# Layer 3's Q, K and V as three fp32r products each, 64-token transposes and 1024-column reads of PSUM in a four-layer model

## The chip, the cores and the metric

The kernel runs on one core of one Trainium2 chip. The metric is the device time of one execution in microseconds. The five engines of a core run their own instruction streams and meet at semaphores: TensorE (PE, with its weight loads as PEld), VectorE (DVE), ScalarE (ACT), GpSimd (POOL) and SyncE (SP), which issues the DMAs.

## What is computed

x is (2, 1024, 256) in float32, 2048 tokens of 256 features. Four layers follow one another: L0 (cumulative attention), L1 (attention and an MLP), L2 (16 heads of 16 features) and L3 (16 heads of 64 features, then a mixture of 8 experts). The change is at the front of L3:

```python
shift = silu(t) @ W_ada.T + b_ada
h = _ln(x, ln1_g, ln1_b) + shift
qkv = (h @ Wqkv.T).reshape(b, n, 3, H, HD)          # H = 16, HD = 64: 3072 columns
q = _ln(qkv[:, :, 0].transpose(0, 2, 1, 3), qn_g, qn_b)
k = _ln(qkv[:, :, 1].transpose(0, 2, 1, 3), kn_g, kn_b)
v = qkv[:, :, 2].transpose(0, 2, 1, 3)
scores = einsum('bhnd,bhmd->bhnm', q, k) / sqrt(HD)
```

## The kernel before

The program is a row of stages with a barrier behind each. `layer3_qkv` (line 1830) is the stage that makes q, k and v of layer 3 and writes them to DRAM for the head stage that follows.

Its start norms and transposes the 2048 tokens in NC = 4 chunks of 512 with `NormTurn` (line 615): VectorE takes mean and variance (`dve_stats`, line 642) and norms (`dve_norm`, 669), TensorE transposes into two banks (`pe_turn`, 681), ScalarE applies gain and shift on the way to `out` (`act_scale`, 690). All four chunks are done before the first product.

Then it goes over T = 16 tiles of 128 tokens. Per tile TensorE makes J + 2 = 6 banks of 512 columns, each of two fp32 products (line 1897, KF = 2 halves of the features): banks 0 and 1 are q, 2 and 3 k, 4 and 5 v. ScalarE copies each q and k bank to `qk` (1924) and squares it into `sq` (1927), and copies v (1932). VectorE sums the squares per head (1964), scales (1965) and inverts (1966), ScalarE takes the root (1934), and VectorE multiplies q and k by it into `xn` (1968). The weights' columns were centred beforehand, so no mean is taken here. In the next tile TensorE transposes `xn` (`turn`, 1883; 16 transposes of 128x128, four to a bank, the two banks 0 and 1 in turn), VectorE applies the head's gain and shift (`gains`, 1958), ScalarE rounds to the fp32r high part `hi` (1917), GpSimd subtracts to get the low part `lo` (1981), and SyncE stores v, hi and lo (1856, 1863). `TURNS` puts the transposes behind banks 3, 4 and 5. `hi`, `lo` and `full` have one buffer per group j of four heads' pairs, so ScalarE waits for the group's stores of the tile before, and VectorE for its `lo`.

The order on an engine is the order in which the code issues. The centring of the weights is done by `CentredWeights` (287) inside layer 2's head stage (`NarrowPairs`, 1331), where SyncE loads `w3qkvT` (302), `w3oT` (303) and `wgateT` (305) after the first two head pairs' loads, and GpSimd centres after it has staged V of SLOTS = 4 pairs (`pool_centre`, called in `pool_program`).

Other stages already use products of parts: a value is hi + lo, both fp32r, and the product is hi x hi + hi x lo + lo x hi, by

```python
PASSES = ((0, 0), (0, 1), (1, 0))
```

for instance in the MLP of layer 1 (line 1112), and the head stage of layer 3 transposes 64 tokens at a time in two row groups (line 1247).

## Time and profile before

| | us |
|---|---|
| runs | 2328.83, 2332.14, 2342.71 |
| median | 2332.14 |
| profiled execution, its own time | 2340.13 |
| its span | 2338.4 |
| mean granted TensorE clock | 0.896 |

Busy over the span: PE 1969.7 us (84%), DVE 1423.3 (61%), ACT 1117.9 (48%), POOL 737.9 (32%). Times in a timeline are us from the span's start. A busy time counts overlapping instructions once; a mean duration holds each instruction's whole latency, so that mean times count can exceed busy. An fp32 product of 512 columns leaves two records. "[n <-X]" is n us of idleness of the engine just before, ended by X.

### The profile page before, as it was taken

To read this page: it belongs to the slowest core of one execution; us is meant where nothing else is said; L and a number is where in the kernel's file an instruction comes from. 1 tells how busy PE (TensorE), PEld (TensorE's weight loads), DVE (VectorE), ACT (ScalarE), POOL (GpSimd) and SP (SyncE) were. 2 spreads that over 40 slices of the span, in tenths; PEclk is the share of its full clock that TensorE was granted. 3 is DMA by queue.
4 is the path that set the end of the run, shared out by engine and by line. 5 is a ranking of instruction groups with operands and counts; after the bars stand their busy time and mean duration, and the time that the engine had idled before them with its cause. 6 is when DMAs were issued, how large, how long until landed. Compare 5 with 4: busy or idle time off the path is not lost. (4 is left out here: it accounts for less than half of the span.)

```text
span 2338.4 us, 34514 instructions
## 1 busy us (share of the span) xinstructions
PE 1969.7 (84%) x12926; PEld 1155.3 (49%) x12926; DVE 1423.3 (61%) x2514; ACT 1117.9 (48%) x2013; POOL 737.9 (32%) x703
## 2 busy tenths in 40 slices
PE   6988589679649999995499949999999999794776
PEld 2444367568323333331345525555555555483676
DVE  5432543453448999960756638777777777317665
ACT  1111133231214888873256538777777777303243
POOL 2221340064003000001235535444444444103476
PEclk8999799889776999995699969999999999895688
DMA  5000000100143211102036783445444444242153
GB/s 158 0 1 0 16 7 1 38 1 1 54 135 99 47 36 49 49 7 77 7 116 216 221 223 86 113 113 113 113 113 111 110 109 109 91 149 103 31 160 81
DMA packets 197254, 190.96 MB, mean 82 GB/s; under 512 B 65440, under 2 KB 155936, under 8 KB 196832
## 3 DMA queue, kind: packets, MB, share of 16 engines
q1 hardware_dynamic: 194016, 184.56, 29.4%
q0 software_dynamic: 3072, 4.20, 0.9%
q8 instruction: 103, 1.69, 0.3%
q14 instruction: 63, 0.52, 0.1%
HBM read 121.07 MB, written 67.37 MB: 81 GB/s over the span
## 5 line engine op out<-in xcount | busy, mean ns | idle before, releaser
L1293 DVE TENSOR_REDUCE l3h_nmax<-l3h_score 128x1 f32<-128x1024 f32 x256 | 313.5, 1225 | 152.7 <-PE l3h_score L1236 152.7
L1327 POOL TENSOR_SCALAR l3h_prob<-l3h_prob,l3h_inv 128x1024 f32<-128x1024 f32 x256 | 288.3, 1126 | 340.6 <-DVE l3h_inv L1299 340.6
L1516 ACT ACTIVATE l2h_pT<-l2h_score 128x512 f32<-128x512 f32 x512 | 266.3, 602 | 118.6 <-PE l2h_score L1441 116.7
L1483 DVE TENSOR_REDUCE l2h_nm<-l2h_rowb 128x1 f32<-128x1024 f32 x256 | 301.0, 1217 | 31.8 <-PE l2h_rowb L1430 31.8
L1317 ACT ACTIVATE l3h_prob<-l3h_score,l3h_nmax 128x1024 f32<-128x1024 f32 x256 | 286.1, 1117 | 48.2 <-DVE l3h_nmax L1293 13.2
L1259 PE MATMUL l3h_out<-l3h_pT,l3h_vs 128*64 128x512 f32 x1024 | 274.4, 617 | 0.0
L1236 PE MATMUL l3h_score<-l3h_K,l3h_Q 64*128 64x512 f32 x1536 | 249.1, 430 | 26.2 <-DMA l3h_K<-l_k 24.3
L1236 PEld LDWEIGHTS l3h_score<-l3h_K,l3h_Q 64*128 64x128 f32 x1536 | 125.8, 186 | 238.0 <-issue 190.1
L1430 PE MATMUL l2h_rowb<-l2h_K,l2h_Q 48*128 48x512 f32 x512 | 183.0, 470 | 40.8 <-DMA l2h_K<-l_k 29.8
L1441 PE MATMUL l2h_score<-l2h_Q,l2h_K 50*128 50x512 f32 x512 | 206.0, 491 | 3.5 <-ACT l2h_pT L1516 3.5
L1285 ACT ACTIVATE l3h_pT<-l3h_ring 128x512 f32<-128x512 f32 x256 | 152.8, 597 | 100.9 <-PE l3h_ring L1247 100.4
L1247 PEld LDWEIGHTS l3h_ring<-ident,l3h_prob 64*128 64x128 f32 x4096 | 172.1, 139 | 37.0 <-issue 8.0
L1897 PE MATMUL l3qkv_bank<-w3qkvT,l3qkv_norm_out 128*128 128x512 f32 x384 | 174.4, 598 | 0.9 <-ACT l3qkv_norm_out L690 0.9
L1430 PEld LDWEIGHTS l2h_rowb<-l2h_K,l2h_Q 48*128 48x128 f32 x512 | 81.4, 199 | 189.1 <-DVE l2h_nm L1483 140.8
L1283 DVE COPY l3h_pT<-l3h_ring 128x512 f32<-128x512 f32 x256 | 172.1, 672 | 2.0 <-PE l3h_ring L1247 2.0
L1247 PE MATMUL l3h_ring<-ident,l3h_prob 64*128 64x64 f32 x4096 | 169.3, 222 | 2.2 <-DVE l3h_pT L1283 1.8
L1453 PE MATMUL l2h_out<-l2h_pT,l2h_vs 128*32 128x512 f32 x1024 | 148.2, 654 | 0.0
L1981 POOL TENSOR_TENSOR l3qkv_lo<-l3qkv_full,l3qkv_hi 128x512 fp32r<-128x512 f32 x64 | 102.3, 1625 | 133.6 <-ACT l3qkv_hi L1917 133.6
L1441 PEld LDWEIGHTS l2h_score<-l2h_Q,l2h_K 50*128 50x128 f32 x512 | 85.8, 195 | 63.3 <-ACT l2h_pT L1516 46.5
L1897 PEld LDWEIGHTS l3qkv_bank<-w3qkvT,l3qkv_norm_out 128*128 128x128 f32 x384 | 70.2, 192 | 72.8 <-issue 71.1
L1528 POOL COPY l2h_vs<-V 128x128 f32<-128x128 f32 x32 | 8.3, 294 | 255.3 <-PE l2h_out L1453 255.3
L1958 DVE TENSOR_SCALAR l3qkv_full<-l3qkv_bank,headln 128x512 f32<-128x512 f32 x64 | 50.5, 808 | 58.6 <-PE l3qkv_bank L1883 40.1
(355 smaller groups left out, 3364.3 us busy)
## 6 DMA issues: line engine op xcount, KB each, us to landing
l3h_Q<-l_q SPq DMA_DIRECT2D x128, 256.0 KB, 4.6
l3h_K<-l_k SPq DMA_DIRECT2D x128, 128.0 KB, 4.9
l_v<-l3qkv_v SPq DMA_DIRECT2D x16, 512.0 KB, 4.1
l_q<-l3qkv_hi SPq DMA_DIRECT2D x32, 256.0 KB, 2.8
l_q<-l3qkv_lo SPq DMA_DIRECT2D x32, 256.0 KB, 2.9
l_k<-l3qkv_hi SPq DMA_DIRECT2D x32, 256.0 KB, 3.7
l_k<-l3qkv_lo SPq DMA_DIRECT2D x32, 256.0 KB, 3.7
l3h_vs<-l_v SPq DMA_DIRECT2D x32, 256.0 KB, 3.5
```

The source lines that it names most:

```text
L1236: mm = pe.matmul(self.score[t % 2][:, c * C:(c + 1) * C], self.Q[r, u, x, t * P:(t + 1) * P], self.K[r, u, y, :], start=i == 0, stop=i == 2)
L1247: mm = pe.transpose(self.ring[half][:, kk * P // 2:(kk + 1) * P // 2], self.prob[r, g % 4, kk * P:(kk + 1) * P], self.ident[r, r])
L1259: mm = pe.matmul(self.ob[n % 2][c * self.hd:(c + 1) * self.hd, :], self.vs[:, n % 2, kk, :], self.pT[:, n % 2, kk, c * C:(c + 1) * C], sta ...
L1283: eng.tensor_copy(dst, src).then_inc(self.emptied_d, 1)
L1293: dve.tensor_reduce(self.nmax[:, t % 4:t % 4 + 1], self.score[t % 2][:, :], AX.X, ALU.max, negate=True).then_inc(self.maxes, 1)
L1317: act.activation(self.prob[:, q, :], self.score[g % 2][:, :], ACT.Exp, bias=self.nmax[:, q:q + 1], accum_out=self.total[:, q:q + 1]).then_ ...
L1327: pool.tensor_scalar(self.prob[:, q, :], self.prob[:, q, :], self.inv[:, q:q + 1], self.vscale, ALU.mult, ALU.mult).then_inc(self.scaled, 1)
L1430: mm = pe.matmul(self.rowb[h][:, c * C:(c + 1) * C], self.Q[r:r + self.SPLIT, u, t * P:(t + 1) * P], self.K[r:r + self.SPLIT, u, c * C:(c ...
L1441: pe.matmul(self.score[v % 3][:, :], self.K[r:r + self.SPLIT + 2, u, k * P:(k + 1) * P], self.Q[r:r + self.SPLIT + 2, u, c * C:(c + 1) * C ...
L1483: dve.tensor_reduce(self.nm[:, mr % 2, at:at + 1], self.rowb[h][:, :], AX.X, ALU.max, negate=True).then_inc(self.maxes, 1)
L1516: act.activation(self.pT[:, g % 4, h, c * C:(c + 1) * C], self.score[v % 3][:, :], ACT.Exp).then_inc(self.exps, 1)
L1897: mm = pe.matmul(bank[2 + j][:, :], nt.out[:, c, kf, t * P:(t + 1) * P], wT[:, (kf * 6 + j) * C:(kf * 6 + j + 1) * C], start=kf == 0, stop ...
```

## The change

- The weights are split: `w3hi` and `w3lo` (fp32r) in place of `w3qkvT`. `CentredWeights` loads one half of the features at a time into `raw`, centres it, and for three pieces of 1024 columns casts to hi and subtracts to lo. The second half and the two other weights are loaded by SyncE at pair 3, and centred before pair 8's staging.
- The normed tokens are split (`NormTurnParts`): ScalarE reads each transposed bank twice (to `out` and to hi), VectorE subtracts to lo. Two chunks come before the first product, the other two in tiles 1 and 3 (`LATER`).
- Each of the 12 fp32 products of a tile becomes three of parts; q, k and v sum in two banks each, and every read of PSUM covers 1024 columns.
- The transposes of `xn` work on 64 tokens at a time in two row groups, into one two-bank tile `turns`: 16 for q, 16 for k.
- VectorE scales the k half of tile tt-1 between inverse and multiply of tile tt, and its q half after the multiply. ScalarE rounds the q half before it copies v, and the k half at the end.
- hi and lo are stored in DMAs of 8 head pairs (512 KB) rather than 4.

TensorE in the middle of a tile, before: products into the banks (`l3qkv_bank<-w3qkvT`), two records' worth at a time, and the transposes (`<-ident,l3qkv_xn`) of the tile before.

```order
L1897 MATMUL l3qkv_bank<-w3qkvT,l3qkv_norm_out 128x512 x2
L1883 MATMUL l3qkv_bank<-ident,l3qkv_xn 128x128 x4
L1897 MATMUL l3qkv_bank<-w3qkvT,l3qkv_norm_out 128x512 x2
L1883 MATMUL l3qkv_bank<-ident,l3qkv_xn 128x128 x8
L1897 MATMUL l3qkv_bank<-w3qkvT,l3qkv_norm_out 128x512 x8
```

And now, from the last k products of tile 1 to its last v products:

```order
L1939 MATMUL l3qkv_k_sum<-w3hi,l3qkv_norm_hi 128x512
L1939 MATMUL l3qkv_k_sum<-w3lo,l3qkv_norm_hi 128x512
L1939 MATMUL l3qkv_k_sum<-w3hi,l3qkv_norm_lo 128x512
L1918 MATMUL l3qkv_turns<-ident,l3qkv_xn 128x64 x16
L1939 MATMUL l3qkv_v_sum<-w3hi,l3qkv_norm_hi 128x512
L1939 MATMUL l3qkv_v_sum<-w3lo,l3qkv_norm_hi 128x512
L1939 MATMUL l3qkv_v_sum<-w3hi,l3qkv_norm_lo 128x512
L1939 MATMUL l3qkv_v_sum<-w3hi,l3qkv_norm_hi 128x512
L1939 MATMUL l3qkv_v_sum<-w3lo,l3qkv_norm_hi 128x512
L1939 MATMUL l3qkv_v_sum<-w3hi,l3qkv_norm_lo 128x512
L1918 MATMUL l3qkv_turns<-ident,l3qkv_xn 128x64 x16
L1939 MATMUL l3qkv_v_sum<-w3hi,l3qkv_norm_hi 128x512
```

The transposes came in three places and four groups; they come in two groups with six v products between them, both into `turns`.

VectorE over one tile, before (`ss` sums of squares, `full` the scaled transposes):

```order
L1964 TENSOR_REDUCE l3qkv_ss<-l3qkv_sq 128x32
L1965 TENSOR_SCALAR l3qkv_rstd<-l3qkv_ss 128x32
L1966 RECIPROCAL l3qkv_rstd<-l3qkv_rstd 128x32
L1968 TENSOR_TENSOR l3qkv_xn<-l3qkv_qk,l3qkv_rstd 128x2048
L1958 TENSOR_SCALAR l3qkv_full<-l3qkv_bank,headln 128x512 x4
```

And now (the first `full` is the k half of the tile before, the second the q half of this one):

```order
L2024 TENSOR_REDUCE l3qkv_ss<-l3qkv_sq 128x32
L2025 TENSOR_SCALAR l3qkv_rstd<-l3qkv_ss 128x32
L2026 RECIPROCAL l3qkv_rstd<-l3qkv_rstd 128x32
L2007 TENSOR_SCALAR l3qkv_full<-l3qkv_turns,headln 128x1024
L2030 TENSOR_TENSOR l3qkv_xn<-l3qkv_qk,l3qkv_rstd 128x2048
L2007 TENSOR_SCALAR l3qkv_full<-l3qkv_turns,headln 128x1024
```

One scaling has moved ahead of the multiply; it waits for TensorE's second group of transposes.

```diff
@@ -291,15 +291,19 @@
...
+        self.raw = s.sb("centre_raw", [P, self.NQ])
...
-    def sp_load(self, sp):
+        self.loaded, self.kept, self.totals, self.means, self.centred, self.rounded, self.rest = (
+            s.sem(f"centre_{n}") for n in ("loaded", "kept", "totals", "means", "centred", "rounded", "rest"))
+
+    def sp_load(self, sp, k):
+        if k >= 1:
+            sp.wait_ge(self.rest, k * 3)
+        sp.dma_start(self.raw[:, :], self.w["WqkvT"][k * P:(k + 1) * P, :]).then_inc(self.loaded, 16)
+
+    def sp_load_rest(self, sp):
         g, w = self.g, self.w
-        for k in range(KF):
-            sp.dma_start(g["w3qkvT"][:, k * self.NQ:(k + 1) * self.NQ], w["WqkvT"][k * P:(k + 1) * P, :]).then_inc(self.loaded, 16)
...
+    def pool_centre(self, pool, k):
+        pool.wait_ge(self.loaded, 16 * (k + 1))
...
+        for i in range(3):
+            at = slice(i * 2 * C, (i + 1) * 2 * C)
+            hi, lo = (self.g[n][:, k * self.NQ + i * 2 * C:k * self.NQ + (i + 1) * 2 * C] for n in ("w3hi", "w3lo"))
+            pool.tensor_copy(hi, self.raw[:, at]).then_inc(self.rounded, 1)
+            pool.wait_ge(self.rounded, 3 * k + i + 1)
+            pool.tensor_tensor(lo, self.raw[:, at], hi.bitcast(F32), ALU.subtract).then_inc(self.rest, 1)
...
-        self.side.sp_load(sp)
+        self.side.sp_load(sp, 0)
         for m in self.TURNS:
+            if m == 3:
+                self.side.sp_load(sp, 1)
+                self.side.sp_load_rest(sp)
...
-            if m == self.SLOTS:
-                self.side.pool_centre(pool)
+            if m in (self.SLOTS, 2 * self.SLOTS):
+                self.side.pool_centre(pool, m // self.SLOTS - 1)
...
+class NormTurnParts(NormTurn):
...
+        self.parts = [s.sb(f"{name}_{n}", [P, NC, KF, C], F32R) for n in ("hi", "lo")]
...
+    def act_scale(self, act, c):
+        b = c * C // S
+        if c >= self.bufs:
+            act.wait_ge(self.split, (c - self.bufs + 1) * KF)
+        for kf in range(KF):
+            act.wait_ge(self.turned, c * KF + kf + 1)
+            for to, sem in ((self.out[:, c % self.bufs, kf, :], self.written), (self.parts[0][:, c, kf, :], self.ready)):
+                act.activation(to, self.banks[kf][:, :], ACT.Identity, bias=self.shift[:, kf, b:b + 1],
+                               scale=self.gain[:, kf, b:b + 1]).then_inc(sem, 1)
+
+    def dve_split(self, dve, c):
+        for kf in range(KF):
+            dve.wait_ge(self.written, c * KF + kf + 1)
+            dve.wait_ge(self.ready, c * KF + kf + 1)
+            dve.tensor_tensor(self.parts[1][:, c, kf, :], self.out[:, c % self.bufs, kf, :],
+                              self.parts[0][:, c, kf, :].bitcast(F32), ALU.subtract).then_inc(self.split, 1)
...
-    HD, QK, J = 64, 2 * H * 64, 4
-    TURNS = {3: (0,), 4: (1,), 5: (2, 3)}
+    HD, W = 64, H * 64
+    LATER = {1: 2, 3: 3}
     with Stage(nc, sems, "l3qkv") as s:
-        X, wT, ident = g["X"], g["w3qkvT"], g["ident"]
-        bank = [s.ps(f"bank{i}") for i in range(8)]
-        nt = NormTurn(s, X, g["gain3"], g["shift3"], ident, bank[0:2], 1e-5, bufs=NC)
-        qk = s.sb("qk", [P, 2, QK])
-        sq = s.sb("sq", [P, QK])
-        xn = s.sb("xn", [P, QK])
+        X, wp, ident = g["X"], (g["w3hi"], g["w3lo"]), g["ident"]
+        tb = s.ps("turns", (P, W))
+        sumb = [s.ps(f"{n}_sum", (P, W)) for n in ("q", "k", "v")]
+        nt = NormTurnParts(s, X, g["gain3"], g["shift3"], ident, [tb[:, kf * C:(kf + 1) * C] for kf in range(KF)], 1e-5)
+        qk = s.sb("qk", [P, 2, 2 * W])
+        sq = s.sb("sq", [P, 2 * W])
+        xn = s.sb("xn", [P, 2 * W])
...
+        full = s.sb("full", [P, 2, W])
+        vsb = s.sb("v", [P, 2, W])
+        hi, lo = s.sb("hi", [P, 2, W], F32R), s.sb("lo", [P, 2, W], F32R)
...
-                        sp.wait_ge(made, n + 1)
...
-                        sp.dma_start(dst[part, n0:n0 + 8, :, at:at + P].rearrange("(j a) d s -> (a d) j s", a=2),
-                                     src[:, j, :].bitcast(F32).rearrange("p (j s) -> p j s", j=4)).then_inc(stored[j], 16)
-            for j in range(J):
-                sp.wait_ge(stored[j], T * 32)
+                        sp.wait_ge(made, 2 * tt + i + 1)
+                        sp.dma_start(g["q3k3"][i][part, b * H:(b + 1) * H, :, at:at + P].rearrange("(j a) d s -> (a d) j s", a=2),
+                                     src[:, i, :].bitcast(F32).rearrange("p (j s) -> p j s", j=8)).then_inc(stored[i], 16)
...
+            def turn(tt, i):
+                n = 2 * tt + i
+                pe.wait_ge(normed, tt + 1)
+                if n >= 1:
+                    pe.wait_ge(fulls, n)
+                for j in range(8):
+                    for h in range(2):
+                        r = slice(h * P // 2, (h + 1) * P // 2)
+                        mm = pe.transpose(tb[:, h * C + j * P // 2:h * C + (j + 1) * P // 2],
+                                          xn[r, i * W + j * P:i * W + (j + 1) * P], ident[r, r])
+                        if j == 7:
+                            mm.then_inc(turned, 1)
+
+            for c in range(2):
                 nt.pe_turn(pe, c)
-            nt.wait_ready(pe, NC - 1)
...
-                        for kf in range(KF):
-                            mm = pe.matmul(bank[2 + j][:, :], nt.out[:, c, kf, t * P:(t + 1) * P],
-                                           wT[:, (kf * 6 + j) * C:(kf * 6 + j + 1) * C], start=kf == 0, stop=kf == KF - 1)
-                        mm.then_inc(sums if j < J else vs, 1)
-                        if tt >= 1 and j in TURNS:
-                            turn(tt - 1, TURNS[j])
-                else:
-                    turn(tt - 1, range(J))
+            nt.wait_ready(pe, 1)
+            for tt in range(T):
+                c, t = divmod(tt, TC)
+                if t == 0:
+                    nt.wait_split(pe, c)
+                for j in range(6):
+                    i, half = divmod(j, 2)
+                    if tt >= 1 and half == 0:
+                        if i < 2:
+                            pe.wait_ge(squared, (tt - 1) * 2 + i + 1)
+                        else:
+                            pe.wait_ge(vc, tt)
+                    for kf in range(KF):
+                        for p_, (x, y) in enumerate(PASSES):
+                            mm = pe.matmul(sumb[i][:, half * C:(half + 1) * C], nt.parts[x][:, c, kf, t * P:(t + 1) * P],
+                                           wp[y][:, (kf * 6 + j) * C:(kf * 6 + j + 1) * C],
+                                           start=kf == 0 and p_ == 0, stop=kf == KF - 1 and p_ == 2)
+                    if half:
+                        mm.then_inc(sums if i < 2 else vs, 1)
+                    if j == 0 and tt in LATER:
+                        pe.wait_ge(fulls, 2 * (tt - 1))
+                        nt.pe_turn(pe, LATER[tt])
+                    if tt >= 1 and j == 3:
+                        if tt in LATER:
+                            nt.wait_ready(pe, LATER[tt])
+                        turn(tt - 1, 0)
+                    if tt >= 1 and j == 4:
+                        turn(tt - 1, 1)
+            for i in range(2):
+                turn(T - 1, i)
...
+            for c in range(2):
+                nt.act_root(act, c)
+                nt.act_scale(act, c)
+
+            def round_hi(tt, i):
+                act.wait_ge(fulls, 2 * tt + i + 1)
+                if tt >= 1:
+                    act.wait_ge(stored[i], tt * 32)
+                act.activation(hi[:, i, :], full[:, i, :], ACT.Copy).then_inc(his, 1)
 
             for tt in range(T):
+                if tt in LATER:
+                    nt.act_scale(act, LATER[tt])
                 if tt >= 2:
                     act.wait_ge(normed, tt - 1)
-                for j in range(J):
-                    act.wait_ge(sums, tt * J + j + 1)
-                    act.activation(qk[:, tt % 2, j * C:(j + 1) * C], bank[2 + j][:, :], ACT.Copy).then_inc(copied, 1)
-                    if tt >= 1 and j == 0:
+                for i in range(2):
+                    act.wait_ge(sums, tt * 2 + i + 1)
+                    act.activation(qk[:, tt % 2, i * W:(i + 1) * W], sumb[i][:, :], ACT.Copy).then_inc(copied, 1)
+                    if tt >= 1 and i == 0:
                         act.wait_ge(ch, 2 * tt)
-                    act.activation(sq[:, j * C:(j + 1) * C], bank[2 + j][:, :], ACT.Square).then_inc(squared, 1)
-                for i in range(2):
-                    act.wait_ge(vs, tt * 2 + i + 1)
-                    if tt >= 2 and i == 0:
-                        act.wait_ge(vstored[tt % 2], tt // 2 * 16)
-                    act.activation(vsb[:, tt % 2, i, :], bank[2 + J + i][:, :], ACT.Copy).then_inc(vc, 1)
+                    act.activation(sq[:, i * W:(i + 1) * W], sumb[i][:, :], ACT.Square).then_inc(squared, 1)
+                    if tt == 0:
+                        nt.act_root(act, 2 + i)
+                if tt >= 1:
+                    round_hi(tt - 1, 0)
+                act.wait_ge(vs, tt + 1)
+                if tt >= 2:
+                    act.wait_ge(vstored[tt % 2], tt // 2 * 16)
+                act.activation(vsb[:, tt % 2, :], sumb[2][:, :], ACT.Copy).then_inc(vc, 1)
                 act.wait_ge(inverse, tt + 1)
                 act.activation(rstd[:, tt % 2, :], rstd[:, tt % 2, :], ACT.Sqrt).then_inc(root, 1)
                 if tt >= 1:
-                    round_hi(tt - 1)
-            round_hi(T - 1)
+                    round_hi(tt - 1, 1)
+            for i in range(2):
+                round_hi(T - 1, i)
...
+            def scaled(tt, i):
+                dve.wait_ge(turned, 2 * (2 * tt + i + 1))
+                if tt >= 1:
+                    dve.wait_ge(los, 2 * (tt - 1) + i + 1)
+                dve.tensor_scalar(full[:, i, :].rearrange("p (j h q) -> p j h q", j=8, h=2),
+                                  tb[:, :].rearrange("p (h j q) -> p j h q", h=2, j=8), g["headln"][:, 2 * i:2 * i + 1],
+                                  g["headln"][:, 2 * i + 1:2 * i + 2], ALU.mult, ALU.add).then_inc(fulls, 1)
+
+            for c in range(2):
+                nt.dve_stats(dve, c)
+                nt.dve_norm(dve, c)
+            for c in range(2):
+                nt.dve_split(dve, c)
+                nt.dve_stats(dve, c + 2)
+            for c in range(2, NC):
+                nt.dve_norm(dve, c)
             for tt in range(T):
                 u = tt % 2
-                dve.wait_ge(squared, (tt + 1) * J)
+                if tt - 1 in LATER:
+                    nt.dve_split(dve, LATER[tt - 1])
+                dve.wait_ge(squared, (tt + 1) * 2)
                 step(dve.tensor_reduce(ss[:, u, :], sq[:, :].rearrange("p (n d) -> p n d", d=HD), AX.X, ALU.add))
                 step(dve.tensor_scalar(rstd[:, u, :], ss[:, u, :], 1.0 / HD, 1e-5, ALU.mult, ALU.add))
                 dve.reciprocal(rstd[:, u, :], rstd[:, u, :]).then_inc(inverse, 1)
+                if tt >= 1:
+                    scaled(tt - 1, 1)
                 dve.wait_ge(root, tt + 1)
                 dve.tensor_tensor(xn[:, :].rearrange("p (n d) -> p n d", d=HD),
                                   qk[:, u, :].rearrange("p (n d) -> p n d", d=HD),
                                   rstd[:, u, :].unsqueeze(2).broadcast_to([P, 2 * H, HD]), ALU.mult).then_inc(normed, 1)
-                gains(tt)
+                scaled(tt, 0)
+            scaled(T - 1, 1)
...
-                for j in range(J):
-                    n = tt * J + j
+                for i in range(2):
                     if tt >= 1:
-                        pool.wait_ge(stored[j], tt * 32)
-                    pool.wait_ge(his, n + 1)
-                    pool.tensor_tensor(lo[:, j, :], full[:, j, :], hi[:, j, :].bitcast(F32), ALU.subtract).then_inc(los, 1)
+                        pool.wait_ge(stored[i], tt * 32)
+                    pool.wait_ge(his, 2 * tt + i + 1)
+                    pool.tensor_tensor(lo[:, i, :], full[:, i, :], hi[:, i, :].bitcast(F32), ALU.subtract).then_inc(los, 1)
...
-                    sb(qkv3, "w3qkvT", [P, KF * 3 * H * 64])
+                    sb(qkv3, "w3hi", [P, KF * 3 * H * 64], F32R)
+                    sb(qkv3, "w3lo", [P, KF * 3 * H * 64], F32R)
```

## Rows read from the trace of the kernel before

**Rows 1.** Window: stretch, length, busy us of PE PEld DVE ACT POOL, clock, DMA share, GB/s.

```profile
1250.00:1300.00 50.00, 50.00 (x167) 25.43 (x166) 33.48 (x33) 30.40 (x63) 27.72 (x18) 1.00 0.71 220
```

**Rows 2.** Timeline of one tile: start us, us, engine, line, what; weight loads left out.

```profile
1264.53 7.03 PE L1897 MATMUL l3qkv_bank<-w3qkvT,l3qkv_norm_out 128*128 128x512 f32 x16
...
1265.75 2.28 DVE L1964 TENSOR_REDUCE l3qkv_ss<-l3qkv_sq 128x32 f32<-128x2048 f32 x1
...
1268.66 0.23 ACT L1934 ACTIVATE l3qkv_rstd<-l3qkv_rstd 128x32 f32<-128x32 f32 x1 [4.20 <-DVE l3qkv_rstd L1966]
1268.80 2.17 ACT L1917 ACTIVATE l3qkv_hi<-l3qkv_full 128x512 fp32r<-128x512 f32 x4
...
1268.92 2.29 DVE L1968 TENSOR_TENSOR l3qkv_xn<-l3qkv_qk,l3qkv_rstd 128x2048 f32<-128x2048 f32 x1 [0.30 <-ACT l3qkv_rstd L1934]
...
1269.55 6.48 POOL L1981 TENSOR_TENSOR l3qkv_lo<-l3qkv_full,l3qkv_hi 128x512 fp32r<-128x512 f32 x4 [5.57 <-ACT l3qkv_hi L1917]
...
1270.88 0.57 ACT L1924 ACTIVATE l3qkv_qk<-l3qkv_bank 128x512 f32<-128x512 f32 x1
...
1271.36 0.58 ACT L1927 ACTIVATE l3qkv_sq<-l3qkv_bank 128x512 f32<-128x512 f32 x1
...
1276.36 1.53 DVE L1958 TENSOR_SCALAR l3qkv_full<-l3qkv_bank,headln 128x512 f32<-128x512 f32 x2 [1.35 <-PE l3qkv_bank L1883]
...
1276.59 7.03 PE L1897 MATMUL l3qkv_bank<-w3qkvT,l3qkv_norm_out 128*128 128x512 f32 x16
```

**Rows 3.** Timeline, the stage's start.

```profile
1147.86 1.40 DVE L642 BATCH_NORM_STATS2 l3qkv_norm_st<-X 128x6 f32<-128x256 f32 x4 [1.15 <-PEq L51]
...
1149.87 1.37 DVE L642 BATCH_NORM_STATS2 l3qkv_norm_st<-X 128x6 f32<-128x256 f32 x4
...
1154.42 1.63 ACT L690 ACTIVATE l3qkv_norm_out<-l3qkv_bank,shift,gain 128x512 f32<-128x512 f32 x2 [2.24 <-PE l3qkv_bank L681]
...
1167.70 19.48 PE L1897 MATMUL l3qkv_bank<-w3qkvT,l3qkv_norm_out 128*128 128x512 f32 x40 [0.87 <-ACT l3qkv_norm_out L690]
...
1178.04 2.29 DVE L1964 TENSOR_REDUCE l3qkv_ss<-l3qkv_sq 128x32 f32<-128x2048 f32 x1 [13.23 <-ACT l3qkv_sq L1927]
```

**Rows 4.** Timeline: the last tile's reduction, and the next stage's first instruction.

```profile
1362.18 2.28 DVE L1964 TENSOR_REDUCE l3qkv_ss<-l3qkv_sq 128x32 f32<-128x2048 f32 x1
...
1386.49 0.49 SPq L1199 DMA_DIRECT2D l3h_Q<-l_q  x1
```

**Rows 5.** Timeline of TensorE in layer 1's MLP: products of parts, one by one.

```profile
474.62 0.63 PE L1112 MATMUL l1mlp_bank<-l1mlp_x_hi,l1mlp_w_hi 128*128 128x512 f32 x1
475.04 0.63 PE L1112 MATMUL l1mlp_bank<-l1mlp_x_lo,l1mlp_w_hi 128*128 128x512 f32 x1
...
476.20 0.39 PE L1112 MATMUL l1mlp_bank<-l1mlp_x_hi,l1mlp_w_lo 128*128 128x512 f32 x1
...
477.79 0.39 PE L1112 MATMUL l1mlp_bank<-l1mlp_x_hi,l1mlp_w_hi 128*128 128x512 f32 x1
```

**Rows 6.** Groups of instructions (busy us, mean ns); L1981: duration ns min/median/max.

```profile
L1247 PE MATMUL l3h_ring<-ident,l3h_prob 64*128 64x64 f32 x4096 | 169.3, 222 | 2.2 <-DVE l3h_pT L1283 1.8
L1317 ACT ACTIVATE l3h_prob<-l3h_score,l3h_nmax 128x1024 f32<-128x1024 f32 x256 | 286.1, 1117 | 48.2 <-DVE l3h_nmax L1293 13.2
L1293 DVE TENSOR_REDUCE l3h_nmax<-l3h_score 128x1 f32<-128x1024 f32 x256 | 313.5, 1225 | 152.7 <-PE l3h_score L1236 152.7
L318 POOL TENSOR_TENSOR l2h_centre_tree<-w3qkvT 128x1024 f32<-128x1024 f32 x2 | 4.7, 2344 | 17.6 <-DMA w3qkvT<-in_L_cond_Wqkv 17.5
L1981 POOL TENSOR_TENSOR l3qkv_lo<-l3qkv_full,l3qkv_hi x64: 1260/1267/2863, 1197.2 to 1378.0; 128x512 fp32r<-128x512 f32 x64
```

**Rows 7.** DMA issues: count, KB each, median us from issue to landing.

```profile
l_k<-l3qkv_lo SPq DMA_DIRECT2D x32, 256.0 KB, 3.7
```

**Rows 8.** Timeline of GpSimd in layer 2's head stage: staging of V for two pairs.

```profile
754.71 0.53 POOL L1528 COPY l2h_vs<-V 128x128 f32<-128x128 f32 x2 [27.69 <-PE l2h_out L1453]
775.90 0.53 POOL L1528 COPY l2h_vs<-V 128x128 f32<-128x128 f32 x2 [20.67 <-PE l2h_out L1453]
```

94 lines of the change are left out of this document (24 added, 70 removed).

## The prediction

> **What bounds the kernel now.** I read the window view first, then the timeline of one tile of the stage that the change rewrites, then the stage's start and end. The stage `layer3_qkv` stands alone between two barriers, so what it gains or loses is the kernel's. The window 1250 to 1300 us [rows 1] shows the reader one full engine, TensorE (50.00 of 50.00 us, granted clock 1.00), beside VectorE at 33.5, ScalarE at 30.4, GpSimd at 27.7 and the DMA engines at 0.71. The timeline [rows 2] shows why: a run of 16 product records starts at 1264.53, the next at 1276.59, so a tile of 128 tokens takes 12.06 us. In it lie 24 product records (two for each of the 12 fp32 products of 512 columns), of which the long run holds 16, and 16 transposes. 16 records run 7.03 us with a tail of some 0.2, so a record costs 0.43 and a product 0.86. 12 x 0.86 = 10.3 us, and the other 1.75 us are transposes, 0.11 each. The sum is the period: TensorE sets it, and nothing else does. ScalarE even waits 4.20 us a tile before its square root [rows 2].
>
> The stage lasts from 1147.86 to 1386.49, the first instruction of the next stage [rows 3, 4]. I cut it in three: 19.84 us to the first product (1167.70) and 10.34 more until VectorE has tile 0's squares (1178.04); 184.14 us for 15 tiles, from 1178.04 to 1362.18; and a tail of 24.31 us.
>
> **The products.** Each fp32 product becomes three of fp32r parts, 36 per tile. The MLP of layer 1 shows this very form (128x128 weights, 512 columns, hi and lo in turn, a new weight load each time): from 476.20 to 477.79 seven starts lie 1.59 us apart, 0.227 us each [rows 5]. So 36 x 0.227 = 8.2 us, against 10.3.
>
> **The transposes.** 16 of 128 tokens become 32 of 64. This form is in the head stage: 4096 records busy for 169.3 us, 0.041 each [rows 6], with the two row halves beside each other. 32 x 0.041 = 1.3 us. TensorE's work is 8.2 + 1.3 = 9.5 us a tile.
>
> **A new wait on TensorE.** All transposes now go through one two-bank tile, `turns`. The k half of tile tt-1 can be transposed only when VectorE has scaled the q half. Between the two stand six v products, 1.37 us. Scaling 1024 columns from PSUM takes as long: 512 columns run at 0.72 (two in 1.53, [rows 2]), and a 1024-column read of PSUM by VectorE, the head stage's maximum, lasts 1.225 [rows 6]; I take 1.25. With 0.3 us for the last transpose and the semaphores TensorE stands some 0.3 us. Behind it are queued the last v products and the next tile's q. Period by TensorE: 9.8 us.
>
> **ScalarE and VectorE.** A second loop runs through both. ScalarE copies and squares q and k (4 instructions of 1024 columns), VectorE reduces and inverts, then, new, scales the k half of the tile before, then ScalarE rounds this to its high part, and only then copies the next q. A 1024-column read of PSUM lasts 1.117 [rows 6]. Back to back they overlap: 1270.88 and 1271.36 start 0.48 apart at 512 columns [rows 2], so I take 1.0. Loop: 4 x 1.0 + 0.1, reduce to root 2.91 (1265.75 to 1268.66), scale 1.25, round 1.05 (half of 2.17), hand-overs 0.3: 9.6 us. Without the second interleaved scaling it would be 8.4. So the new order puts this loop just under TensorE's 9.8, and either may set the tile. ScalarE's own work is 7.3 us and VectorE's 7.8, inside the period.
>
> **GpSimd and the port.** The low parts become two subtractions of 1024 columns. A 1024-column TENSOR_TENSOR takes 2.34 [rows 6]. Four of 512 took 1.27 each except the one beside VectorE's two-input multiply `xn`: 2.86 at most [rows 6], starting at 1269.55, and `xn` itself still took 2.29 [rows 2]. So 4.7 us of work, plus a wait of 1.1 us behind `xn` for the k half. The q half's subtraction now lies beside the reduction; no row here shows that pair, so its extra cost is between 0 and a full 2.28 us. I take 0, because GpSimd's median beside VectorE's other work stayed at 1.27. Even 2.28 more ends before `xn` does. The Trainium skill (SBUF — State Buffer, "Who interferes with whom") has the rule that a VectorE instruction with two SBUF inputs contends with GpSimd's reads and a tensor_reduce never does, and that whoever starts first holds the port. The first half agrees with the 2.86; by the rule my 0 stands, but the order in which `xn` and a subtraction start could turn against `xn`, which is the second rival.
>
> **The stores.** Same bytes and same 512-byte pieces, in 5 DMAs a tile instead of 9. At a share of 0.71 [rows 1] they need 12.06 x 0.71 = 8.6 us, so 88% of 9.8: not the bound. The single `hi` and `lo` buffer per half must be stored before ScalarE rounds the next tile: round 1.05, wait for `xn` 1.1, subtract 2.34, hand-overs 0.1, landing. A 256 KB k store lands in 3.7 us [rows 7]; 256 KB more at this rate are 0.9, so 4.6, together 9.2 us, under 9.8 with 0.6 to spare.
>
> **The stage's start.** The stats pass of a chunk is 2.0 us (1147.86 to 1149.87, [rows 3]). Now two chunks instead of four are normed before the first product, and each bank is read twice (out and hi), each chunk's lo made by VectorE. ScalarE gets chunk 0 at 1154.42 [rows 3], 6.6 us after the start. It comes a stats pass earlier, 4 activations at 0.82 (1.63 for two) make 3.3, then TensorE's first bank of chunk 1 1.2, 3.3 more: first product some 12.4 us after the start, 7.4 earlier. Bounds: 0.5 per activation gives 10, a wait on the split 15. The chunks left out come back inside tiles 1 and 3: TensorE waits for its transposed tile to be scaled and for four activations. Going through the waits tile by tile, tile 3 loses 3.3 us and tile 1 about 1.1 (the fulls of tile 1 exist only after tile 2's inversion, 4 us into tile 3's slot. TensorE reaches tile 3's wait 1 us into it, and the transposes, activations and hand-over behind the wait run beside the q and k products.) Cost 4.4; bounds 0 and 9.
>
> **The tail.** 24.3 us now: 16 transposes and four reads in turn, then stores one behind the other. With halves of 1024 columns the same chain is 6.8 us to `xn`, 0.8 + 1.3 + 1.1 for q, 0.8 + 1.3 + 1.1 + 2.4 for k, partly waiting on stores, and 4 for the last landing: 21. Gain 3, bounds 0 and 5.
>
> **Layer 2's head stage** gets the splitting of the weights: 6 casts and 6 subtractions on GpSimd, and half of the loads at pair 3 instead of at the start. GpSimd idles 20.67 us of every 21.19 us pair and stages a pair's V three pairs ahead [rows 8]; 15 to 30 us more each time are hidden by that. SyncE's three later loads precede the stores and shifts of pair 3, which are due 10 us on. I cost it at 0; without the cover at most 5 us.
>
> **The sum.** Start -7.4; 15 tiles 184.1 to 15 x 9.8 + 4.4 = 151.4, so -32.7; tail -3. Total -43 us. The profiled execution took 2340.13, so it would take 2297. It lies 8 us above the median of the runs, 2332.14, from which the same sum gives 2289. The time asked for is that of such runs: I say 2290.
>
> **Rivals.**
> (a) The stores' loop sets the tile: landing grows to 7 us as 512 KB DMAs queue behind v. Period 1.05 + 1.1 + 2.34 + 0.1 + 7 = 11.6, +27: 2317. For it: only 0.6 us of slack and a share of 0.88. Against it: v is issued behind the k half, not ahead.
> (b) GpSimd holds the port first and `xn` waits: up to 2.4 less 0.7 of slack a tile, 11.5, +25: 2315. Against it: counted from the squares, the q half's subtraction runs from 1.1 to 3.5 us and `xn` starts at 2.91 + 1.25 = 4.2, 0.7 later.
> (c) Slower: TensorE, no longer full (it stands 0.3 to 3 us at a time), is granted 0.5, the lower of its two levels (1.2 and 2.4 GHz), through the stage. Starts at 474.62 and 475.04 are 0.42 apart [rows 5], which is 512 columns at 1.2 GHz, so 36 x 0.42 + 2.6 = 17.8 us a tile, +5.7 against before: 16 x 5.7 - 10 = +81, 2413. It decides from a mean granted clock below 9.5 / 12.7 = 0.75. Against it: now the stage shows 1.00, and waits of 0.3 us are small beside 9.5. The Trainium skill (TensorE: Matmul & The Clock Gate, "HAM oscillation — how this bites in real kernels") says that gaps in the work bring the lower level back; the longest here come at tile 3. That page and the rows differ only in how much idleness is left, so its price is (c)'s.
> (d) The change does more: both loops at TensorE's floor of 9.5, no loss in tiles 1 and 3, a start of 10 us: -4.5 -4.4 -2.4, 2279.
>
> **How the numbers follow.** Forecast 0.80, (a) 0.06, (b) 0.06, (c) 0.03, (d) 0.05. About 1% is what a measurement of this kernel can tell from no change: 2309 and 2355 here. The forecast and (d) lie below 2309, and a little of (a) and (b), less a slice of the forecast in which the period is 11: faster 0.87; same 0.10; slower 0.03. The range takes (d) with the runs' scatter of some 7 us, 2272, and on the other side (a) and (b), 2318.
>
> **What would show it.** In the changed profile: tiles 9.8 us apart with TensorE over 95% busy at clock 1.00; product starts 0.227 apart; 1024-column reads near 1.1 us on ScalarE and 1.34 on VectorE; first product 12 us into the stage; a gap of 3 us in tile 3; the stage 195 us long instead of 238.6; layer 2's head stage unchanged. I am wrong if the tile is over 11 us (look at who releases ScalarE's rounding: a DMA is (a)), if `xn` is over 2.3 us (b), or if the clock falls (c).

## The result, and the profile after

The changed kernel took 2304.4 us (median of 4 runs, 2299.20 to 2307.17), the kernel before 2331.4 beside it (median of 4). The ratio is 0.987 with a 95% interval of 0.985 to 0.989: faster by 1.3%. The forecast was 2290 with a range of 2272 to 2318. The sign and the range held. The gain is some 30 us where 43 were forecast.

The profiled execution of the changed kernel took 2303.45 us. The stage `layer3_qkv`, by the rows that answer to [rows 3, 4]:

```profile
1149.68 1.41 DVE L651 BATCH_NORM_STATS2 l3qkv_norm_st<-X 128x6 f32<-128x256 f32 x4 [1.15 <-PEq L51]
...
1157.31 0.21 ACT L668 ACTIVATE l3qkv_norm_rstd<-l3qkv_norm_rstd 128x4 f32<-128x4 f32 x1
1157.56 1.38 DVE L678 TENSOR_SCALAR l3qkv_norm_xn<-X,l3qkv_norm_mv,l3qkv_norm_rstd 128x256 f32<-128x256 f32 x4 [2.11 <-ACT l3qkv_norm_rstd L668]
...
1162.98 0.79 PE L1939 MATMUL l3qkv_q_sum<-w3hi,l3qkv_norm_hi 128*128 128x512 f32 x1 [2.02 <-ACT l3qkv_norm_hi L1857]
...
1172.92 1.38 DVE L678 TENSOR_SCALAR l3qkv_norm_xn<-X,l3qkv_norm_mv,l3qkv_norm_rstd 128x256 f32<-128x256 f32 x4 [1.40 <-ACT l3qkv_norm_rstd L668]
...
1174.22 2.28 DVE L2024 TENSOR_REDUCE l3qkv_ss<-l3qkv_sq 128x32 f32<-128x2048 f32 x1
...
1349.76 0.49 SPq L1208 DMA_DIRECT2D l3h_Q<-l_q  x1
```

The stage lasts 1349.76 - 1149.68 = 200.08 us against 238.63. The first product comes after 13.30 us (19.84 before), the first reduction 11.24 later (10.34), the last reduction stands at 1326.96, so 15 tiles take 152.74 (184.14), and the tail is 22.80 (24.31). From the next stage's first instruction to the end of the span both kernels take 951.9 us. The window that answers to [rows 1] (same columns):

```profile
1250.00:1300.00 50.00, 50.00 (x340) 38.64 (x339) 43.09 (x30) 35.06 (x40) 27.67 (x10) 1.00 0.83 260
```

TensorE is still full, at clock 1.00. One tile, in the columns of [rows 2], most product rows left out:

```profile
1253.92 0.40 PE L1939 MATMUL l3qkv_k_sum<-w3hi,l3qkv_norm_lo 128*128 128x512 f32 x1
1254.25 0.71 PE L1918 MATMUL l3qkv_turns<-ident,l3qkv_xn 64*128 64x64 f32 x16
1254.89 0.51 PE L1939 MATMUL l3qkv_v_sum<-w3hi,l3qkv_norm_hi 128*128 128x512 f32 x1
1255.23 0.39 PE L1939 MATMUL l3qkv_v_sum<-w3lo,l3qkv_norm_hi 128*128 128x512 f32 x1
...
1256.15 0.40 PE L1939 MATMUL l3qkv_v_sum<-w3hi,l3qkv_norm_lo 128*128 128x512 f32 x1
1256.33 2.29 DVE L2024 TENSOR_REDUCE l3qkv_ss<-l3qkv_sq 128x32 f32<-128x2048 f32 x1
1256.41 1.06 ACT L1966 ACTIVATE l3qkv_hi<-l3qkv_full 128x1024 fp32r<-128x1024 f32 x1
...
1256.52 0.71 PE L1918 MATMUL l3qkv_turns<-ident,l3qkv_xn 64*128 64x64 f32 x16
...
1257.50 0.39 PE L1939 MATMUL l3qkv_v_sum<-w3lo,l3qkv_norm_hi 128*128 128x512 f32 x1
...
1257.61 2.40 POOL L2043 TENSOR_TENSOR l3qkv_lo<-l3qkv_full,l3qkv_hi 128x1024 fp32r<-128x1024 f32 x1 [1.66 <-ACT l3qkv_hi L1966]
...
1258.65 1.40 DVE L2025 TENSOR_SCALAR l3qkv_rstd<-l3qkv_ss 128x32 f32<-128x32 f32 x1
...
1260.36 1.25 DVE L2007 TENSOR_SCALAR l3qkv_full<-l3qkv_turns,headln 128x1024 f32<-128x1024 f32 x1
...
1261.52 2.28 DVE L2030 TENSOR_TENSOR l3qkv_xn<-l3qkv_qk,l3qkv_rstd 128x2048 f32<-128x2048 f32 x1
1261.64 1.06 ACT L1966 ACTIVATE l3qkv_hi<-l3qkv_full 128x1024 fp32r<-128x1024 f32 x1 [0.93 <-DVE l3qkv_full L2007]
...
1266.42 2.29 DVE L2024 TENSOR_REDUCE l3qkv_ss<-l3qkv_sq 128x32 f32<-128x2048 f32 x1
```

Reductions stand 10.09 us apart, ten times in a row; 9.8 was forecast. A surprise lies in it: VectorE's `tensor_scalar` of 128x32 at 1258.65 takes 1.40 us, and ends when GpSimd's subtraction of the q half (1257.61, 2.40 us) does. In the stage's first tile, with GpSimd idle, it takes 0.18. One can walk a closed loop by these rows: reduction 2.3, the blocked instruction 1.4, reciprocal 0.3, scaling 1.3, rounding 1.0, four reads at 0.95, and the next reduction, 10.09 later. So two engines fit the period, and a busy share doesn't say which of them sets it. That was the first question for the chip.

The second was layer 2's head stage, forecast to be free. The stage before layer 3 has one long pair. Its rows, first GpSimd's and VectorE's, then the windows (the columns of [rows 1]):

```profile
829.90 3.62 POOL L327 TENSOR_TENSOR l2h_centre_raw<-l2h_centre_raw,l2h_centre_mean 128x2048 f32<-128x2048 f32 x1
...
830.32 3.23 DVE L1502 CAST l2h_nm_parts<-l2h_nm 128x16 fp32r<-128x16 f32 x1
...
834.03 5.21 SPq L1415 DMA_DIRECT2D l2h_Q<-l2h_shift  x8
...
835.16 0.49 PE L1442 MATMUL l2h_rowb<-l2h_K,l2h_Q 48*128 48x512 f32 x1 [3.52 <-DVE l2h_nm L1495]
```

```profile
827.00:831.00 4.00, 4.00 (x27) 1.24 (x27) 3.72 (x4) 3.36 (x7) 3.52 (x7) 1.00 0.00 0
831.00:835.00 4.00, 0.65 (x4) 0.21 (x4) 3.93 (x4) 1.09 (x2) 3.86 (x3) 1.00 0.00 0
835.00:839.00 4.00, 3.84 (x20) 1.85 (x20) 2.84 (x4) 1.97 (x4) 3.92 (x3) 0.66 0.02 3
839.00:843.00 4.00, 4.00 (x18) 1.57 (x17) 2.29 (x3) 2.00 (x5) 3.92 (x3) 0.50 0.01 1
843.00:847.00 4.00, 4.00 (x27) 1.21 (x26) 3.81 (x4) 3.31 (x7) 0.97 (x1) 0.98 0.24 64
```

VectorE's cast of a pair's maxima, 0.17 us in the other pairs, takes 3.23 beside GpSimd's centring of the second half of the weights. Behind it on VectorE stands the first reduction of the next maxima (`l2h_nm`), which frees the bank that TensorE fills next. So TensorE stands from 831.64 to 835.16, and then runs at a granted clock of 0.66 and 0.50 until 843. GpSimd's stagings of V are 26.63 us apart there (823.22 and 849.85) and 21.23 from one pair to the next in the steady part: 5.4 us lost, in a term that I had at 0.

### The profile page after: what moved, and what is told of

Read it like the earlier page. It is cut to its first block and busy times, and to the rows that moved or that the text cites. A ratio compares the mean times of both kernels' runs of the same rounds, so it can differ in the third digit from the quotient of the medians.

```text
span 2301.7 us, 35109 instructions
## 1 busy us (share of the span) xinstructions
PE 1931.4 (84%) x13374; PEld 1181.4 (51%) x13374; DVE 1435.9 (62%) x2490; ACT 1116.1 (48%) x1909; POOL 739.2 (32%) x683
## 5 line engine op out<-in xcount | busy, mean ns | idle before, releaser
L2043 POOL TENSOR_TENSOR l3qkv_lo<-l3qkv_full,l3qkv_hi 128x1024 fp32r<-128x1024 f32 x32 | 88.9, 2778 | 109.3 <-ACT l3qkv_hi L1966 109.3
L1705 PE MATMUL l3o_bank<-w3oT,l3o_oT 128*128 128x256 f32 x256 | 57.9, 391 | 13.0 <-DMA l3o_oT<-l_heads_out 13.0
L2419 PE MATMUL moe_up<-moe_gT_hi,moe_w1T_hi 128*128 128x256 f32 x128 | 42.9, 335 | 29.8 <-DVE moe_gT_lo L2499 24.8
L505 PE MATMUL l_bank<-l_csum,l_val 128*128 128x512 f32 x128 | 64.2, 626 | 4.0 <-DVE l_aT L590 4.0
```

## The experiments

All times of a stage are from the profile of each kernel; "tile" is the distance of two reductions in the steady part. Except for e8, each edit is made to the changed kernel alone. e1, e4 and e5 leave out terms of the products and serve for their times only.

**e1: two products of parts in place of three.** The loop over the passes in this stage:

```diff
-for p_, (x, y) in enumerate(PASSES):
+for p_, (x, y) in enumerate(((0, 0), (1, 0))):
```

> The product of the tokens' high parts with the weights' low parts is left out in layer 3's Q, K and V: 24 products a tile in place of 36. In the changed kernel the tiles stand 10.09 us apart. Theory 'port': the period is a loop of ScalarE and VectorE (reduction 2.29, tensor_scalar 1.40 behind GpSimd's subtraction, reciprocal 0.35, scaling 1.25, rounding, two copies and two squares), and TensorE has room. Then the period stays 10.1 us although 12 x 0.232 = 2.8 us of TensorE's work go. Rival 'TensorE': 8.35 of products, 1.4 of transposes and its waits set the tile, as the prediction had it; then the period falls to 8 or 9 us.

Measured: tile 9.82 us, its small `tensor_scalar` 1.18. 2.8 us of TensorE's work went, and only 0.27 came back. So TensorE's products had a part in the 10.09, and a second bound stands at 9.82, just under it.

**e2: GpSimd's subtraction in two halves.**

```diff
-pool.tensor_tensor(lo[:, i, :], full[:, i, :], hi[:, i, :].bitcast(F32), ALU.subtract).then_inc(los, 1)
+for a in range(2):
+    at = slice(a * W // 2, (a + 1) * W // 2)
+    ins = pool.tensor_tensor(lo[:, i, at], full[:, i, at], hi[:, i, at].bitcast(F32), ALU.subtract)
+ins.then_inc(los, 1)
```

> GpSimd's subtraction of 1024 columns (2.40 us) in layer 3's Q, K, V becomes two of 512; nothing else. Theory 'port': VectorE's tensor_scalar of 128x32 (1.40 us in place of 0.18) asks about 1 us after GpSimd's start and would find the port free after the first half, some 0.2 us later; it lasts under 0.5 us, the loop is 9.1 to 9.3 us, and the period falls from 10.09 to what TensorE needs, 9.6 to 9.8. If GpSimd's second half takes the port first, tensor_scalar stays at 1.4 and the period at 10.1. Rival 'TensorE': the period stays at 10.1 whatever tensor_scalar does.

VectorE's chain in one tile of e2:

```profile
1255.09 2.29 DVE L2024 TENSOR_REDUCE l3qkv_ss<-l3qkv_sq 128x32 f32<-128x2048 f32 x1
1257.41 0.30 DVE L2025 TENSOR_SCALAR l3qkv_rstd<-l3qkv_ss 128x32 f32<-128x32 f32 x1
1257.74 0.35 DVE L2026 RECIPROCAL l3qkv_rstd<-l3qkv_rstd 128x32 f32<-128x32 f32 x1
...
1263.88 1.34 DVE L2007 TENSOR_SCALAR l3qkv_full<-l3qkv_turns,headln 128x1024 f32<-128x1024 f32 x1 [2.42 <-PE l3qkv_turns L1918]
1265.17 2.29 DVE L2024 TENSOR_REDUCE l3qkv_ss<-l3qkv_sq 128x32 f32<-128x2048 f32 x1
```

The block is gone (0.30 in place of 1.40), and the tile is 10.09 all the same (two in these rows are 10.08 apart). The 1.1 us reappear as a wait for TensorE's transposes, 2.42 in place of 1.32. So the blocked instruction doesn't set the tile.

**e3: the `tensor_scalar` goes into the root.** On VectorE, the reciprocal moves behind the wait for the root; on ScalarE, the root reads the sums:

```diff
-step(dve.tensor_scalar(rstd[:, u, :], ss[:, u, :], 1.0 / HD, 1e-5, ALU.mult, ALU.add))
-dve.reciprocal(rstd[:, u, :], rstd[:, u, :]).then_inc(inverse, 1)
...
 dve.wait_ge(root, tt + 1)
+step(dve.reciprocal(rstd[:, u, :], rstd[:, u, :]))
...
-act.activation(rstd[:, tt % 2, :], rstd[:, tt % 2, :], ACT.Sqrt).then_inc(root, 1)
+act.activation(rstd[:, tt % 2, :], ss[:, tt % 2, :], ACT.Sqrt, bias=eps[:, 0:1],
+               scale=1.0 / HD).then_inc(root, 1)
```

> VectorE's tensor_scalar (x/64 + 1e-5) in layer 3's Q, K, V goes into ScalarE's square root (scale 1/64, bias 1e-5), and the reciprocal follows the root. Chain now reduction, root 0.20, reciprocal, xn; the scaling of the k half starts straight behind the reduction. Theory 'port': the loop loses 1.40 + 0.35, 8.4 us, the period is TensorE's, 9.6 to 9.8 us; 15 tiles x 0.4 = 6 us less for the stage. The reciprocal or the scaling may wait for the port in its place; then one of these lasts over 1 us longer. Rival 'TensorE': 10.1.

Tile 10.09 again. 15 tiles take 151.18 (152.74), and the gain is all in the first three. The stage is 197.51, 2.6 us shorter where 6 were expected. "Rival TensorE" held, here and in e2.

**e4: e1 and e3 together.**

> e3 and e1 together: the tensor_scalar goes into the root, and the product of high tokens with low weights is left out. Theory 'port': with both TensorE's work (7.0 us) and the blocked tensor_scalar gone, the period is the bare loop, 8.3 to 8.8 us. If a third thing held the tile (GpSimd's two subtractions 5.6, the stores 9.2 by the prediction's sum), the period stays over 9.2.

```profile
1253.13 2.28 DVE L2029 TENSOR_REDUCE l3qkv_ss<-l3qkv_sq 128x32 f32<-128x2048 f32 x1
...
1256.70 0.34 DVE L2033 RECIPROCAL l3qkv_rstd<-l3qkv_rstd 128x32 f32<-128x32 f32 x1
...
1261.57 2.29 DVE L2029 TENSOR_REDUCE l3qkv_ss<-l3qkv_sq 128x32 f32<-128x2048 f32 x1
```

About half of the steady tiles take 8.44 us and a little over, the others 9.3 to 9.6, and the mean is 8.9: there ScalarE's rounding waits for a store (7.1 us in the stage for the low parts of k, against 1.9 in the changed kernel, all of it in the last tile). The stage is 182.16 us. In order, the bounds are: TensorE's floor 10.09, the loop with the block 9.82, the stores' loop (rival (a) of the prediction) at 9.3 to 9.6 in some tiles, and the loop without the block and the reciprocal 8.4.

**e5: fp32 products with all else kept.**

```diff
-for p_, (x, y) in enumerate(PASSES):
-    mm = pe.matmul(sumb[i][:, half * C:(half + 1) * C], nt.parts[x][:, c, kf, t * P:(t + 1) * P],
...
+mm = pe.matmul(sumb[i][:, half * C:(half + 1) * C], nt.parts[0][:, c, kf, t * P:(t + 1) * P].bitcast(F32),
+               wp[0][:, (kf * 6 + j) * C:(kf * 6 + j + 1) * C].bitcast(F32),
+               start=kf == 0, stop=kf == KF - 1)
```

> Undoes the three products alone: one fp32 product of the rounded high parts (12 instructions, 24 records a tile) in place of 36 of high and low parts; the low parts are left out of the sum. The runs so far say that TensorE sets the changed tile: 36 x 0.232 = 8.35 and twice 0.87 around the transposes, 10.09. Theory 'TensorE': 24 records at 0.43 are 10.3, and with the transposes 11.7 to 12.1 us a tile, the 12.06 of the kernel before, so that all the gain inside the tile is the products'. Rival 'shared gain': the 64-token transposes, the wide evictions and VectorE's order have a part in it; then the tile stays under 11.4.

Tile 11.98 us, stage 228.31. Of the 38.55 us by which the stage is shorter, 28.2 are the products'. They are 26.3 in the 15 tiles and 1.9 between the first product and the first reduction. Of the other 10.3 us 3.7 lie in the start, 5.1 in the tiles (in the kernel before, the first two reductions alone stand 15.38 us apart) and 1.5 in the tail.

**e6: transposes of 128 tokens.**

```diff
-for h in range(2):
-    r = slice(h * P // 2, (h + 1) * P // 2)
-    mm = pe.transpose(tb[:, h * C + j * P // 2:h * C + (j + 1) * P // 2],
-                      xn[r, i * W + j * P:i * W + (j + 1) * P], ident[r, r])
+mm = pe.transpose(tb[:, j * P:(j + 1) * P], xn[:, i * W + j * P:i * W + (j + 1) * P], ident[:, :])
```

VectorE's scaling then reads `tb` in plain order.

> Undoes the transposes alone: 8 of 128 tokens for each half in place of 16 of 64. In the kernel before 4 of them stood 0.11 apart: 8 take 0.87, 16 small ones 0.64. In the changed kernel each group costs TensorE 0.87 altogether (1253.92 to 1255.23 without two product pitches), so some 0.2 of it is at the turns from product to transpose and back. Theory 'TensorE': 2 x 0.23 more, 10.55 us a tile. Rival: the turn costs nothing with 128-token transposes (none was seen in the kernel before), 10.1. If the tile is not TensorE's, 10.09 to the hundredth.

```profile
1253.81 0.40 PE L1936 MATMUL l3qkv_k_sum<-w3hi,l3qkv_norm_lo 128*128 128x512 f32 x1
1254.05 1.03 PE L1916 MATMUL l3qkv_turns<-ident,l3qkv_xn 128*128 128x128 f32 x8
1254.84 0.48 PE L1936 MATMUL l3qkv_v_sum<-w3hi,l3qkv_norm_hi 128*128 128x512 f32 x1
1255.16 0.39 PE L1936 MATMUL l3qkv_v_sum<-w3lo,l3qkv_norm_hi 128*128 128x512 f32 x1
```

And at the tile's second place:

```profile
1255.12 1.35 DVE L2004 TENSOR_SCALAR l3qkv_full<-l3qkv_turns,headln 128x1024 f32<-128x1024 f32 x1 [1.70 <-PE l3qkv_turns L1916]
```

```profile
1256.08 0.40 PE L1936 MATMUL l3qkv_v_sum<-w3hi,l3qkv_norm_lo 128*128 128x512 f32 x1
1256.62 1.07 PE L1916 MATMUL l3qkv_turns<-ident,l3qkv_xn 128*128 128x128 f32 x8
```

Tile 10.47 us, stage 204.84, 4.8 over the changed kernel. Of the 0.38 us a tile the form itself is little: the first place costs 1.35 less two product pitches, 0.89, against 0.85 with the small transposes, and the scaling lasts as long (1.35 for 1.34). The rest is a wait for VectorE at the second place. There the transposes begin 0.54 behind the last product, where 0.24 are enough at the first place, so 0.3 us are lost. They begin 0.15 us behind the end of the scaling of the q half (1256.47). In the changed kernel the same 0.15 lie between the scaling's end (1256.37) and the transposes (1256.52), but its last product pitch ends at 1256.38, so that its wait is 0.04 at most. The small transposes gain by ending sooner: their scaling starts 1.11 us behind the last k product, and 1.31 with the large ones.

**e7: both scalings behind `xn`, as before.**

```diff
-if tt >= 1:
-    scaled(tt - 1, 1)
...
 scaled(tt, 0)
+scaled(tt, 1)
```

> Undoes VectorE's order alone: both scalings stand behind xn. The chain from xn by q's transposes (0.7), scaling 1.3, k's transposes 0.7, scaling 1.3 then ends before the next reduction starts. Theory 'TensorE': the period stays 10.09, since VectorE has 7.9 us of work and the loop of ScalarE (reduction, root, rounding, four reads) loses the scaling of the k half, 1.25, and is under 9.3. Rival 'order matters': the k half is scaled only behind TensorE's second transposes, the reduction behind it starts late, and the tile takes 10.5 to 12 us; then the new order is worth that much.

In the steady part "TensorE" holds: tile 10.09, so the order brings nothing there. But the tiles 1 to 5 take 59.0 us in place of 51.8, and the stage 205.53. In these rows of its third tile VectorE stands for the transposes that the next tile's products and the late chunk hold up:

```profile
1197.90 2.29 DVE L2028 TENSOR_TENSOR l3qkv_xn<-l3qkv_qk,l3qkv_rstd 128x2048 f32<-128x2048 f32 x1 [0.30 <-ACT l3qkv_rstd L1988]
1202.32 1.34 DVE L2007 TENSOR_SCALAR l3qkv_full<-l3qkv_turns,headln 128x1024 f32<-128x1024 f32 x1 [2.13 <-PE l3qkv_turns L1918]
1205.82 1.34 DVE L2007 TENSOR_SCALAR l3qkv_full<-l3qkv_turns,headln 128x1024 f32<-128x1024 f32 x1 [2.16 <-PE l3qkv_turns L1918]
1207.08 2.27 DVE L2024 TENSOR_REDUCE l3qkv_ss<-l3qkv_sq 128x32 f32<-128x2048 f32 x1
```

The tail gives 2.0 back (20.84): the last `xn` starts 3.18 us behind its reduction and not 5.16, since neither the scaling of tile 14's k half nor a blocked instruction stands between. So the order is worth 5.5 us, 7.3 in the tiles less some 2 in the tail.

**e8: the kernel before, profiled again.**

> The kernel before, unchanged, profiled a second time. In its first profile layer 2's head stage ends with 40 us at a granted TensorE clock of 0.50 (1045 to 1085), where the changed kernel's has 20, and the profiled execution took 2340.1, 8 us over the median. Theory 'clock': those 8 us lie there; a second profile whose time is at the median, 2330 to 2333, has at most some 20 us at 0.50 there, and the last maxima to last store of that stage take about 40 us and not 49. Rival: the 8 us lie elsewhere, or a profile at the median shows 49 too.

The windows of the kernel before (its first profile, then e8):

```profile
1045.00:1065.00 20.00, 18.70 (x62) 4.59 (x60) 0.00 (x0) 10.98 (x21) 0.00 (x0) 0.50 0.03 8
1065.00:1085.00 20.00, 18.96 (x66) 4.90 (x66) 0.00 (x0) 9.39 (x18) 0.00 (x0) 0.50 0.00 0
```

```profile
1045.00:1065.00 20.00, 16.46 (x95) 4.74 (x87) 0.00 (x0) 16.08 (x32) 0.00 (x0) 1.00 0.04 9
1065.00:1085.00 20.00, 8.47 (x51) 2.22 (x51) 1.75 (x1) 8.69 (x16) 1.36 (x3) 0.84 0.19 55
```

e8 took 2332.6, at the median, and the stretch from the last pair's maxima to layer 3's start took 96.0 us in place of 110.2 (the cast of the maxima at 1042.48 and 1037.66, layer 3's first instruction at 1138.52 and 1147.86). The rest of e8 was 6.6 us longer than in the first profile, in several small pieces. The granted clock falls at about 1042 us in the first profile and 1079 in e8. So two profiles of the same code differ by 14 us there, and by their rows it is when the clock falls. In the 12 profiles of changed kernels the stretch took 94.0 to 102.8 us (101.6 in the changed kernel's own, 94.7 in e10, with the same code in that stage).

**e9: the weights' work placed between the maxima.** GpSimd's centring and rounding, for each half, wait until VectorE has transposed a pair's maxima; the second load follows one pair later. `PIECES` is (3, 4, 7, 8), and the pieces are centring and rounding of the first half, then of the second.

```diff
-if m in (self.SLOTS, 2 * self.SLOTS):
-    self.side.pool_centre(pool, m // self.SLOTS - 1)
...
 ins.then_inc(self.staged, 1)
+if m in self.PIECES:
+    pool.wait_ge(self.turned, m)
+    self.side.pool_piece(pool, self.PIECES.index(m))
```

> Layer 2's head stage alone: GpSimd's centring (9.9 us) and its rounding of the weights (10.3 us), for each half, become four pieces, each behind the transpose of a pair's maxima on VectorE, so that none is under way when VectorE takes the next pair's maxima apart, 21 us later. In the changed kernel one pair lasts 26.63 us in place of 21.23, where VectorE's cast of 128x16 lasted 3.23 us beside GpSimd's subtraction of 3.62. Theory 'port': every pair is 21.2 to 21.3 us long, the stage and with it the kernel are 5 to 6 us shorter than the changed kernel, 2298 to 2300. Rival 'reload': the second half of the weights, read from memory beside the heads' loads, held the pair; then one pair still lasts over 24 us. Rival 'start': the first 5 us of the stage's start gain too, where GpSimd no longer stands beside VectorE's first maxima: 1 us more.

Every pair from the third on is 21.20 to 21.25 us, the long one is gone, and 2295.5 us were measured (ratio 0.983, 0.980 to 0.987), where 2298 to 2300 were expected. The interval overlaps with the changed kernel's, 0.985 to 0.989, so the gain is read from the pairs. Whether the first pairs gained is not shown: the first took 24.05 us for 25.14, but the other profiles with the changed kernel's code there have 24.08 to 25.46. From the first pair's maxima to the last's it takes 322.4 us (328.95 in the changed kernel, 323.0 in e8): 6.5 us are the pairs'. Of the 8.9 us between the medians 2.4 are left; the stretch behind the pairs differs by more than that between profiles of the same code.

**e10: products start on the first chunk.**

```diff
-for c in range(2):
-    nt.pe_turn(pe, c)
-nt.wait_ready(pe, 1)
+nt.pe_turn(pe, 0)
...
+if j == 0 and tt == 0:
+    nt.pe_turn(pe, 1)
```

The last two lines stand behind the tile's first six products. VectorE splits chunk 0 ahead of norming chunk 1.

> Layer 3's Q, K, V: the first tile's products wait for the first chunk's parts alone, and the second chunk's transposes stand behind six of them. In the changed kernel the first product starts 13.3 us into the stage (forecast 12.4), waiting for the second chunk, whose normalization stood 2.11 us for a root queued behind ScalarE's scaling of the first. Theory: first product at 9 to 10 us, first reduction 3 to 4 us sooner (24.5 us now), the tiles unchanged, stage 3 to 4 us shorter. Rival: the chunk's transposes, scaling and normalization only move into tile 0 and the first reduction comes at the same time, within 1 us; or TensorE stays at its low clock for longer and gives it back.

First product 8.60 us into the stage (13.30), first reduction 21.45 (24.54), stage 197.19, 2.9 shorter. The one run took 2294.4 us; the other 7 us under the changed kernel's median are not this edit's, since the stretch before layer 3 is 7 us shorter in it.

**e11: e3, e9 and e10 together.**

> The changed kernel with e3 (eps in the root), e9 and e10 together, all of the computation kept. TensorE sets the tile, so e3 adds 1 us at most; e9 5 to 6 and e10 3 to 4 us add up, since they lie in two stages: 2293 to 2296 us against 2304 of the changed kernel and 2331 of the kernel before. If the granted clock in the last pairs of layer 2's head stage falls at another time, some 5 us either way.

2287.5 us (median of 6, 2282 to 2297) where 2293 to 2296 were expected, ratio 0.981 with 0.978 to 0.984, below the changed kernel's 0.985 to 0.989. The stage takes 194.20 us. This version beats both kernels, by 45 and by some 17 us, with the whole computation kept.

**e12: the centring in four pieces, at its old place.**

```diff
-pool.tensor_tensor(qk, qk, self.mean[:, :].unsqueeze(2).broadcast_to([P, 2 * H, self.HD]),
-                   ALU.subtract).then_inc(self.centred, 1)
+for i in range(4):
+    at = slice(i * H // 2, (i + 1) * H // 2)
+    ins = pool.tensor_tensor(qk[:, at, :], qk[:, at, :],
+                             self.mean[:, at].unsqueeze(2).broadcast_to([P, H // 2, self.HD]), ALU.subtract)
+ins.then_inc(self.centred, 1)
```

> In layer 2's head stage GpSimd's subtraction of the means (2048 columns, 3.62 us) becomes four of 512; where it stands, the loads and the rounding stay as in the changed kernel. There VectorE's cast of 128x16 asked 0.42 us after its start and lasted 3.23 us, TensorE stood from 831.5 to 835.2 and then ran at a granted clock of 0.66 and 0.50 until 843, and the pair was 5.4 us long over the others. Theory 'port, then clock': the cast waits for the first piece at most and lasts under 1.2 us, TensorE's gap is under 2 us, the clock stays at 1.00, and the pair is 21.3 to 22.3 us, so 4 to 5 us go. Rival 'port alone': the gap shrinks by what the cast does, but the clock falls all the same, 23 to 24 us. Rival 'reload of the weights' or GpSimd's work as a whole (e9 moved both): still over 25 us. If the later pieces take the port one behind the other ahead of VectorE, the cast stays at 3 us and the pair at 26.

```profile
827.71 4.04 POOL L329 TENSOR_TENSOR l2h_centre_raw<-l2h_centre_raw,l2h_centre_mean 128x512 f32<-128x512 f32 x4
```

```profile
828.10 0.68 DVE L1505 CAST l2h_nm_parts<-l2h_nm 128x16 fp32r<-128x16 f32 x1
828.82 0.97 DVE L1507 TENSOR_TENSOR l2h_nm_parts<-l2h_nm,l2h_nm_parts 128x16 fp32r<-128x16 f32 x1
```

```profile
831.00:835.00 4.00, 3.81 (x28) 1.39 (x28) 3.78 (x5) 2.70 (x6) 3.86 (x3) 1.00 0.02 3
835.00:839.00 4.00, 4.00 (x31) 1.53 (x23) 3.49 (x4) 2.91 (x6) 3.92 (x4) 1.00 0.01 1
```

The cast and the subtraction behind it each wait for one piece, 1.3 us together; TensorE stands for 1.8 us; the clock stays at 1.00; the pair is 22.53 us, 1.3 over the others and 0.2 over the range expected. With loads and rounding where they were, this leaves the reload out as a cause. Of the 5.4 us, 3.1 are the block's (3.23 less 0.17) and 2.3 are left for the clock that fell behind the gap.

**The runs together.** "Pair" is the distance in layer 2's head stage between VectorE's casts for the sixth and the seventh head pair, the long one; "stretch" goes from the cast for the last head pair to layer 3's first instruction.

| kernel | us (runs) | stage | pair | stretch |
|---|---|---|---|---|
| before | 2331.4 (4) | 238.63 | 21.22 | 110.2 |
| changed | 2304.4 (4) | 200.08 | 26.63 | 101.6 |
| e1 | 2298.6 (1) | 195.33 | 27.42 | 101.5 |
| e2 | 2304.0 (1) | 199.76 | 26.18 | 102.8 |
| e3 | 2303.3 (1) | 197.51 | 26.65 | 101.9 |
| e4 | 2283.5 (1) | 182.16 | 28.87 | 100.3 |
| e5 | 2327.6 (1) | 228.31 | 26.08 | 98.2 |
| e6 | 2307.9 (1) | 204.84 | 26.64 | 102.0 |
| e7 | 2307.9 (1) | 205.53 | 26.65 | 101.5 |
| e8, before again | 2332.6 (1) | 239.36 | 21.22 | 96.0 |
| e9 | 2295.5 (4) | 199.85 | 21.23 | 94.1 |
| e10 | 2294.4 (1) | 197.19 | 25.74 | 94.7 |
| e11 | 2287.5 (6) | 194.20 | 21.24 | 94.0 |
| e12 | 2300.5 (4) | 199.97 | 22.54 | 102.6 |

Up to e7, and in e10, layer 2's code is the changed kernel's, and pair and stretch still differ between profiles. So what an edit does in layer 3 is read from the stage, not from the time of a single run.

The table also tests the split of the 5.4 us. Nine profiles have the changed kernel's code in this stage. In all of them the cast lasts 3.21 to 3.25 us and TensorE stands for 3.51 to 3.54, but the pair takes from 25.74 us (e10) to 28.87 (e4). What it loses beyond the block goes with the time that TensorE then spends at a granted clock of 0.50: 1.5 us for 3.4 us at 0.50 (e10), 2.3 for 6.8 (changed kernel), 3.1 for 8.6 (e1), 4.6 for 12.7 (e4). So the block has one price, and the clock adds 0.34 to 0.43 of the time that it is low, a time that differs from execution to execution.

## Why the prediction came out as it did

**The products: right.** Starts 0.232 us apart for 0.227, so 8.35 us a tile for 8.2. e5 prices them at 1.89 us a tile and 28.2 for the stage, nearly three quarters of its gain.

**The transposes: mis-sized.** The pitch was right: 16 run from 1254.25 to 1254.89, 0.64. But the place around them costs more. From 1253.92 to 1255.23 are 1.31 us for two products, which take 2 x 0.232, so 0.85 us are the transposes' and not 0.64; the second place of the tile (1256.15 to 1257.50) costs 0.89. Product to transpose is 0.33 and not 0.23, and so is the first product behind. This is 0.45 us a tile that no step of mine had, since the rows that I took the prices from [rows 5, 6] show each form in long runs of its own.

**A new wait on TensorE: too large.** The 0.3 us are not there, or 0.04 of them (0.37 from product to transpose at the second place, 0.33 at the first). e6, where 0.3 us are lost at this place, shows how near it was. 8.35 + 0.85 + 0.89 = 10.09 is the period; 9.8 was 8.2 + 1.3 + 0.3. The errors partly cancel, and 0.29 us a tile are left, 4.4 over 15.

**ScalarE and VectorE: right by luck.** 9.6 was forecast and e1 shows 9.82, "just under TensorE". But "reduce to root 2.91" was 4.1, from 1256.33 to 1260.47, for the block at the port, and the rest was shorter than summed: without the block and the reciprocal it is 8.4 (e4).

**GpSimd and the port: asked of the wrong instructions.** I took 0 for the q half's subtraction beside the reduction, and looked at `xn` alone for a price. The reduction is indeed not touched (2.29), `xn` neither (2.28). The small instruction behind the reduction was, by 1.2 us a tile; e2 shows that TensorE hid it. The Trainium skill (SBUF — State Buffer, "Who interferes with whom") puts a copy, a cast and a `tensor_scalar` among the operations that can take the shared pair of ports, and says that whoever issues first keeps it for the whole instruction. The 1.40 and the 3.23 agree with it. Rival (b) is seen once in a row of e4, where `xn` took 3.16, and not in the changed kernel.

**The stores, rival (a): right.** ScalarE waits 1.9 us for them in the whole stage, in its last tile, and they show up first when the tile could be 8.4 us (e4).

**The start: 12.4 forecast, 13.3 measured.** The difference is the second chunk's root, which stands on ScalarE behind four scalings of the first and holds VectorE for 2.11 us (1157.56). e10 shows that the wait for the second chunk was not needed at all. From the first product to the first reduction I had kept the 10.34 us of before, without a reason; it took 11.24. The squares are done at 1172.80, but VectorE norms the fourth chunk first (1172.92), and reduces at 1174.22. So the start gave 5.6 us and not 7.4. The chunks that come back in tiles 1 and 3 cost 1.4 us (the first five tiles take 51.8, and 5 x 10.09 are 50.5), not 4.4: I had given TensorE no earlier slack, where tiles 1 and 5 took 9.51 and 8.92. This gives back 3.0 of the 4.4 that the period cost, so that 15 tiles took 152.7 for 151.4.

**The tail: 22.8 for 21.3.** Its parts were not tried apart, but its rows can be set beside mine: `xn` ends 7.45 us behind the reduction (6.8 forecast; the block is in it), from there to the last store's issue at 1343.50 are 9.1 (8.8), and from this to the next stage 6.3, where I had 4. I had allowed 1.7 for waits. Together the start gave 5.6 for 7.4, the tiles 31.4 for 32.7 and the tail 1.5 for 3, or 38.6 us of the 43.

**Layer 2's head stage "at 0": the step that failed.** I asked whether GpSimd has time, and it has, 20 us in each pair. I didn't ask what VectorE does at the shared port in that time, and what TensorE does after a gap. The price was 5.4 us, over the 5 that I had as a bound, and 4.5 to 7.6 in the nine profiles. The Trainium skill (TensorE: Matmul & The Clock Gate, "HAM oscillation — how this bites in real kernels") says that gaps in the work bring the lower level back. The windows agree: 0.50 after 3.5 us of standing. In the prediction I weighed that rule for layer 3 alone.

**The sum.** 38.55 - 5.4 = 33 us, against 27 by the medians and 30 by the ratio (25 to 35 by its interval). Profile by profile the account closes. Between e8, which ran at the median of the kernel before, and the changed kernel's profile are 29.2 us: 39.3 from the stage, less 5.9 in the pairs, less 5.6 in the stretch behind them (96.0 to 101.6), and 1.4 elsewhere. Whether the 5.6 belong to the change is not shown: the kernel before has 96.0 and 110.2 in its two profiles, the changed kernel's code 94.7 to 102.8 in nine. The same stretch is why the first profile of before stood 8 us over its median: I saw the distance and carried it along correctly, but not its place.

## What to carry to other kernels

When two engines fit a period, take work from each alone and from both: 10.09, 9.82 and 8.4 were told apart by e1 to e4, not by the first profile. Work put on an idle engine is priced by what it holds (a port, a buffer) while a short instruction on a critical chain asks for it; long instructions there should be cut or placed behind that chain. Here a gap of 3.5 us on TensorE cost its length and, on top, 0.34 to 0.43 of the time at the lower clock that followed. Ahead of a forecast, look in which stretch the profiled execution differs from the median.

## What the runs showed of the hardware

- VectorE's 128x32 `tensor_scalar` and 128x16 cast, 0.18 and 0.17 us, lasted 1.40 and 3.23 beside one subtraction of GpSimd, to the end of that subtraction. Where GpSimd's work came in pieces, VectorE got the port between two of them: 0.30 (e2), and 0.68 and 0.97 for two instructions in a row (e12). VectorE's reduction and its `xn` were not held in the changed kernel (2.29 and 2.28).
- TensorE lost 0.1 us from the last product to the first of the 64-token transposes, and 0.1 behind the first product that followed them. With 128-token transposes (e6) nothing was lost ahead (1253.81 to 1254.05) and 0.09 behind. So 16 small ones, 0.15 us faster from first start to next product than 8 large ones (0.64 against 0.79), came out 0.04 cheaper in their place.
- In layer 2's head stage, whose steady pairs otherwise ran at 1.00, a gap of 3.5 us was followed by 3.4 to 12.7 us at a granted clock of 0.50 in nine profiles of the same code; with a gap of 1.8 us (e12) the clock stayed at 1.00. For the last pairs of the stage, where TensorE has less to do, it fell at about 1042 us in one profile of the kernel before and at 1079 in the other.
